# Score units of a head pair side by side in six PSUM banks, transposes over four banks, Q and K projected together

## What is computed

```python
h = layernorm(x) * (1 + ca) + sa
q, k, v = h @ W_Q, h @ W_K, h @ W_V              # 16 heads of 64
probs = softmax(where(causal, -1e6, q @ k.T / 8))
x = x + ga * ((probs @ v) @ W_out + b_out)
h = layernorm(x) * (1 + cb) + sb
x = x + gb * top2_of_8_experts(h)                # 128 -> 512 -> 128, gelu
```

## Time and profile before

| what | value |
|---|---|
| median of three runs | 2189.81 us (2189.57 to 2190.14) |
| profiled execution | 2190.27 us, span 2188.5 us |
| TensorE busy | 2047.3 us, 94% of the span |
| VectorE busy | 1700.8 us, 78% |
| ScalarE busy | 1531.4 us, 70% |
| GpSimd busy | 722.2 us, 33% |
| granted TensorE clock, mean | 0.994 |

### The profile page before, as it was taken

How to read it: one execution, slowest core, us unless ns; L and a number is a source line. 1 busy time by engine, 2 the same in 40 slices (tenths; PEclk the granted TensorE clock), 3 DMA queues, 4 the chain that set the end, 5 groups by cost and what they waited for, 6 DMA issues and landing times. The chain is left out here.

```text
span 2188.5 us, 45861 instructions
## 1 busy us (share of the span) xinstructions
PE 2047.3 (94%) x12751; PEld 1550.8 (71%) x12751; DVE 1700.8 (78%) x4517; ACT 1531.4 (70%) x3749; POOL 722.2 (33%) x1215
## 2 busy tenths in 40 slices
PE   5999999999999999999999999879999999999998
PEld 3676666666666666667666667568888888888887
DVE  5877767777777677777777777579999888898887
ACT  4777667667677676676677767567776777676775
POOL 2334334333333333333343434212222222222222
PEclk9999999999999999999999999989999999999999
DMA  3000000000000000000000000031211112111111
GB/s 109 16 1 1 0 1 1 0 0 1 0 1 0 1 1 0 1 1 0 1 0 0 1 0 1 1 116 47 75 50 47 43 43 69 56 48 43 43 47 45
DMA packets 41996, 49.99 MB, mean 23 GB/s; under 512 B 3176, under 2 KB 23712, under 8 KB 41888
## 3 DMA queue, kind: packets, MB, share of 16 engines
q1 hardware_dynamic: 41632, 48.41, 7.0%
q0 software_dynamic: 256, 0.53, 0.1%
HBM read 44.47 MB, written 4.46 MB: 22 GB/s over the span
## 5 line engine op out<-in xcount | busy, mean ns | idle before, releaser
L340 POOL TENSOR_SCALAR probs<-probs,rdenom 128x512 f32<-128x512 f32 (+3 forms) x1024 | 522.4, 532 | 840.6 <-DVE rdenom L694 840.6
L564 ACT ACTIVATE probs<-probs,neg_max 128x512 f32<-128x512 f32 (+3 forms) x1024 | 562.8, 553 | 287.2 <-DVE neg_max L685 287.2
L685 DVE CUSTOM_DVE_ANT_0 probs<-banks,mask_w 128x512 f32<-128x512 f32 (+3 forms) x1024 | 441.0, 485 | 66.7 <-PE banks L398 53.5
L1005 ACT ACTIVATE hidden<-banks,b_cols 128x512 f32<-128x512 f32 x512 | 348.4, 685 | 198.5 <-PE banks L871 172.9
L1124 DVE TENSOR_TENSOR hid_lo<-hidden,hid_hi 128x512 fp32r<-128x512 f32 x512 | 386.7, 763 | 67.5 <-ACT hid_hi L1013 55.2
L427 PE MATMUL banks<-ident,probs 128*128 128x128 f32 x2560 | 392.2, 280 | 46.4 <-DVE z_lo L698 34.0
L427 PEld LDWEIGHTS banks<-ident,probs 128*128 128x128 f32 x2560 | 289.7, 141 | 154.0 <-DVE probs_T L674 50.7
L943 POOL TENSOR_TENSOR acc<-acc,y_w 128x512 f32<-128x512 f32 x112 | 155.1, 1385 | 489.5 <-DVE y_w L1137 489.5
L439 PE MATMUL banks<-probs_T,v_sb 128*64 128x512 f32 (+3 forms) x2048 | 303.9, 439 | 1.6 <-DVE probs_T L674 1.6
L674 DVE COPY probs_T<-banks 128x512 f32<-128x512 f32 x384 | 261.7, 681 | 55.4 <-PE banks L427 54.6
L439 PEld LDWEIGHTS banks<-probs_T,v_sb 128*64 128x64 f32 x2048 | 136.0, 137 | 152.4 <-issue 124.2
(11 more groups left out here) (138 smaller groups left out, 3506.2 us busy)
## 6 DMA issues: line engine op xcount, KB each, us to landing
w_rows<-w_kept SPq DMA_DIRECT2D x128, 256.0 KB, 3.9
x_all<-in_L_attn_resid_dram SPq DMA_DIRECT2D x16, 256.0 KB, 2.6
out_dram<-y_result SPq DMA_DIRECT2D x16, 256.0 KB, 2.3
w_raw<-in_L_ffn_W_dram SPq DMA_DIRECT2D x12, 256.0 KB, 4.0
hidden<-in_L_ffn_W_dram SPq DMA_DIRECT2D x4, 256.0 KB, 6.3
v_sb<-in_L_attn_W_Q_dram SPq DMA_DIRECT2D x1, 512.0 KB, 6.0
v_sb<-in_L_attn_W_K_dram SPq DMA_DIRECT2D x1, 512.0 KB, 8.1
v_sb<-in_L_attn_W_V_dram SPq DMA_DIRECT2D x1, 512.0 KB, 11.2
```

Of the source, the lines that this page charges most:

```text
L340: pool.tensor_scalar(part, part, rdenom[:, p % 2, 4 * h + r:4 * h + r + 1], 1.0, ALU.mult, ALU.mult)\
L564: act.activation(part, part, ACT.Exp, bias=neg_max[:, p % 2, col:col + 1], scale=-1.0, accum_out=denom[:, p % 2, col:col + 1]).then_inc(p_ ...
L685: dve.tensor_tensor_reduce(out=probs[:, p % 2, h, at:at + n], in0=s_banks[S_BANK[u] + h][:, col:col + n], in1=mask_w[:, 512 - n:512], scal ...
L1005: act.activation(hidden[:, e % 2, c, :], banks[:, c, :], ACT.Gelu, bias=b1_cols[:, e * HC + c:e * HC + c + 1]).then_inc(hid, 1)
```

## The change

The three score units of a pair get six banks of their own: unit 0 `s_banks[0:2]`, unit 1 `s_banks[2:4]`, unit 2 `z_bank` and `g_bank`. The transposes go in turn over four banks: T0 `g_bank`, T1 `s_banks[0]`, T2 `s_banks[1]`, T3 `z_bank`, T4 `g_bank`. The order on TensorE in a pair becomes: unit 0, unit 2, unit 1, weighting, [output projection], T0, Q, K, [attention_T], T1, T2, V, T3, V, T4. VectorE masks unit 2, then 0, then 1, and ScalarE takes the exponentials in that order; q_lo and k_lo, and q_hi and k_hi, stand next to each other. The V chunks move: pair 2 has none, pair 5 has one. The waits follow the banks: scores wait for the copies of the transposes, transposes T0 to T2 and the weighting for the masks of the pair under way.

```diff
-S_BANK = [0, 2, 0]
-V_CHUNKS = [[0, 1], [2, 3], [4], [5, 6], [7], [], [], []]
+V_CHUNKS = [[0, 1], [2, 3], [], [4, 5], [6], [7], [], []]
-    return (h, 2 + 2 * h, 6 + h)[u]
+    return (2 + h, 4 + 2 * h, h)[u]
-        T_BANK = [g_bank, z_bank, g_bank, z_bank, g_bank]
+        T_BANK = [g_bank, s_banks[0], s_banks[1], z_bank, g_bank]
+        S_BANK = [s_banks[0:2], s_banks[2:4], [z_bank, g_bank]]
...
# TensorE, scores(b, p, u, begin, young)
+                            if not young:
+                                pe.wait_ge(t_act, pair(2, b, p) - 3)
+                                pe.wait_ge(t_dve, pair(3, b, p) - 4)
-                        if u == 2:
-                            pe.wait_ge(s_masked, pair(8, b, p) + 2)
+                        if u == 2 and not young:
+                            pe.wait_ge(t_act, pair(2, b, p) - 2)
+                            pe.wait_ge(t_dve, pair(3, b, p) - 3)
...
# TensorE, transposes(b, p, u, begin, step)
-                        if u == 0 and not begin:
-                            pe.wait_ge(t_dve, pair(3, b, p))
-                        if u == 1 and not begin:
+                        if u < 3 and step is not None:
+                            pe.wait_ge(s_masked, pair(8, *step) + 2 + u)
+                        if u == 3 and not begin:
                             pe.wait_ge(z_done, pair(1, b, p))
-                        if u == 2:
+                        if u == 4:
                             pe.wait_ge(t_dve, pair(3, b, p) + 1)
-                        if u == 3:
-                            pe.wait_ge(t_act, pair(2, b, p) + 1)
-                        if u == 4:
-                            pe.wait_ge(t_dve, pair(3, b, p) + 2)
...
# TensorE, the body of a pair
-                            scores(b, p, 0, begin)
+                            scores(b, p, 0, begin, young)
+                            scores(b, p, 2, begin, young)
...
-                            scores(b, p, 1, begin)
+                            scores(b, p, 1, begin, young)
+                            if not young:
+                                weigh_values(*prev2, (b, p))
                             if p == 2 and not first:
                                 project_out(b - 1)
-                            if not (first and p < 2):
-                                weigh_values(*prev2)
-                            scores(b, p, 2, begin)
...
                             if not begin:
-                                transposes(*prev, 0, first and p == 1)
+                                transposes(*prev, 0, young, (b, p))
                             if has_next:
                                 project_q(*nxt)
-                            if not begin:
-                                transposes(*prev, 1, first and p == 1)
...
                             if has_next:
                                 project_k(*nxt)
+                            if p == 4 and not first:
+                                attention_T(b - 1, pair(8, b, p) + 8)
                             if not begin:
-                                transposes(*prev, 2, False)
+                                transposes(*prev, 1, young, (b, p))
+                                transposes(*prev, 2, young, (b, p))
...
# ScalarE, the body of a pair
-                            exponentials(b, p, 0, 0)
-                            exponentials(b, p, 1, 0)
+                            for u in (2, 0):
+                                for h in range(2):
+                                    exponentials(b, p, h, u)
...
# VectorE, the body of a pair
-                            mask_and_max(b, p, 0, early)
-                            mask_and_max(b, p, 1, early)
+                            for u in (2, 0, 1):
+                                mask_and_max(b, p, u, early)
...
-                            mask_and_max(b, p, 2, early)
                             if not begin:
                                 evac_T(*prev, 0, first and p == 1)
                             if has_next:
                                 rest_q(*nxt)
+                                rest_k(*nxt)
+                            if p == 4 and not first:
+                                add_attention(b - 1)
                             if not begin:
                                 evac_T(*prev, 2, False)
-                            if has_next:
-                                rest_k(*nxt)
```

More of the change, by code:

```diff
@@ L375, in h_transposes, with scores @@
                         for t in range(NT):
-                            mm = pe.transpose(s_banks[2][:, t * P:(t + 1) * P], xn[:, t, :], ident[:, :])
+                            mm = pe.transpose(s_banks[3][:, t * P:(t + 1) * P], xn[:, t, :], ident[:, :])
                         mm.then_inc(lnT_ps, 1)
-                    def scores(b, p, u, begin):
+                    def scores(b, p, u, begin, young):
                         if u == 0:
@@ L397, in scores @@
                                     own = slice(h * DH, (h + 1) * DH)
-                                    mm = pe.matmul(s_banks[S_BANK[u] + h][:, at:at + n], q[own, p % 2, rows],
+                                    mm = pe.matmul(S_BANK[u][h][:, at:at + n], q[own, p % 2, rows],
                                                    k[own, p % 2, 0:n], start=start, stop=stop)
@@ L407, in _, with transposes @@
                                [(h, 2, r, 256 * h + (r - 2) * P) for h in range(2) for r in (2, 3)]]
-                    def transposes(b, p, u, begin):
+                    def transposes(b, p, u, begin, step=None):
                         if u == 0:
@@ L428, in transposes, with weigh_values @@
                         mm.then_inc(t_ps, 1)
-                    def weigh_values(b, p):
+                    def weigh_values(b, p, step=None):
+                        if step is not None:
+                            pe.wait_ge(s_masked, pair(8, *step) + 1)
                         pe.wait_ge(t_dve, pair(3, b, p) + 3)
@@ L446, in values @@
                         t, half = i % 4, i // 4
-                        pe.wait_ge(s_masked, pair(8, b, p) + 6)
+                        pe.wait_ge(s_masked, pair(8, b, p) + 8)
                         toks, cols = slice(t * P, (t + 1) * P), slice(half * 512, half * 512 + 512)
@@ L477, in body @@
                         for p in range(NP):
[L478 removed]
+                            begin, young = first and p == 0, first and p < 2
                             has_next = not (last and p == NP - 1)
                             prev, prev2, nxt = before(b, p), two_before(b, p), after(b, p)
[L481 removed]
+                            scores(b, p, 0, begin, young)
+                            scores(b, p, 2, begin, young)
                             if p > 0 and V_CHUNKS[p - 1]:
@@ L509, in body @@
                             if p == 5 and not last:
-                                pe.wait_ge(s_masked, pair(8, b, p) + 6)
+                                pe.wait_ge(s_masked, pair(8, b, p) + 8)
                                 h_transposes(b + 1)
                             if not begin:
-                                transposes(*prev, 3, False)
+                                transposes(*prev, 3, young, (b, p))
                             if len(V_CHUNKS[p]) > 1:
                                 values(b, p, 1)
-                            if p == 4 and not first:
-                                attention_T(b - 1, pair(8, b, p) + 6)
                             if not begin:
-                                transposes(*prev, 4, False)
+                                transposes(*prev, 4, young, (b, p))
                     end = B - 1
@@ L676, in mask_and_max @@
                     def mask_and_max(b, p, u, early):
-                        if u == 0 and not early:
+                        if u == 2 and not early:
                             wait_alone(dve, t_ps, pair(5, b, p) - 5)
-                        wait_alone(dve, s_ps, pair(3, b, p) + u + 1)
+                        wait_alone(dve, s_ps, pair(3, b, p) + (1, 3, 2)[u])
                         for h in range(2):
@@ L727, in body @@
                             has_next = not (last and p == NP - 1)
-                            mask_and_max(b, p, 0, early)
-                            mask_and_max(b, p, 1, early)
+                            for u in (2, 0, 1):
+                                mask_and_max(b, p, u, early)
                             if p == 2 and not first:
                                 gate_attention(b - 1)
-                            if not (first and p < 2):
+                            if not early:
                                 rest_z(*two_before(b, p))
-                            mask_and_max(b, p, 2, early)
                             if not begin:
@@ L747, in body @@
                                 evac_T(*prev, 4, False)
-                            if p == 4 and not first:
-                                add_attention(b - 1)
```

16 lines of the change are left out of this document (7 added, 9 removed).

## The result

The changed kernel takes 2155.24 us (median of four, 2151.86 to 2161.79); the kernel before, run beside it, took 2189.97 (2189.57 to 2191.0). The ratio is 0.9842 [0.9822, 0.9861]: faster by 34.7 us, where 15.9 were forecast, and the time lies under the lower end of the range. The sign and the waits came out as written; the size is off by more than half.

A forecast was written before the change was run, and what follows sets the result against it. TensorE's work was taken to bound pairs with V, a chain over three engines those without. Savings of 12.6 us in the loop, 0.9 in the unrolled batches and 2.4 in the drain total 15.9, giving 2174 us, range 2158 to 2198.

The forecast's parts named there:

- TensorE's own work: TensorE in every pair: moving score units and weighting costs nothing by itself; a pair with two V chunks takes 9.76 us.
- The jump: Pair 0: VectorE's first mask (M) starts 2.30 us after its last copy, 2.83 after unit 0's start (S); pair 0 takes 10.90.
- The release and the mask's start: Pair boundary: waits release in 0.14 us (ends 0.04, 0.24); first mask starts 0.22 after unit 2's issue, up to 0.32.
- z_lo's hole: TensorE before transposes: the 34.0 us wait goes, as z_hi and z_lo get more than two us of cover.
- the waits for k_lo: TensorE before scores, 31.9 us: K is projected before T1, so k_lo is never late because of TensorE.
- The slots of the chain: ScalarE and VectorE, from a pair's first mask (M): q_hi at M+5.31, k_lo M+6.54, T4's copy ends M+8.51.
- Pair 4: Next batch's normalisation ahead of the masks, residual sum (0.61) before T2's copy: first mask at 2.54, pair 11.13 us.
- the normalisation: VectorE in pair 4, ahead of the masks: the next batch's normalisation takes 1.91 us in four pieces.
- The longer chain: Rival, slower: the mask-to-copy round of pairs 2, 4, 5, 6, 7 and the jump exceeds its slots; 0.35 gives 2204; chance 0.14.
- the rival of no change: Rival at the pair boundary: release 0.24 and mask start 0.32 together take 18 us, giving 2185 to 2194; chance 0.15.
- TensorE's work bounds all: Rival, much faster: k_lo and copies never late, pairs 6 and 7 take 8.32; 73 us less, 2116; chance 0.05.
- The clock: Rival: holes in and before pair 0 drop TensorE's clock to 0.52, costing 27 us over fourteen batches: 2201; chance 0.06.

The follow-up runs named there:

- the two moves together: Layer norm into VectorE's holes and pair 4's residual sum behind T4's copy, against the changed kernel: 2133.89 us, ratio 0.9747 to the kernel before.
- the last kernel: On the two moves together: h's subtraction behind T4's copy in pair 6, T4 ahead of the second V chunk; 2117.14 us, ratio 0.9662 to the kernel before.

## Why the prediction was right in kind and wrong in size

**TensorE's own work: the step that failed, a cost put at nothing.** "Moving them costs nothing by itself: the number and size of the instructions stay." They stay, and their cost doesn't. Pair 3 of the change has two V chunks and no hole worth the name, as pair 1 had before (K of that pair, and what follows it, in the first two lines; then the change):

```profile
643.99 0.48 PE L350 MATMUL banks<-h_hi,wk_hi 128*128 128x512 f32 x1
...
644.78 0.66 PE L427 MATMUL banks<-ident,probs 128*128 128x128 f32 x4
```

```profile
654.11 0.50 PE L403 MATMUL banks<-k_hi,q_hi 64*128 64x512 f32 x2 [0.26 <-DVE probs_T L677]
...
654.91 0.29 PE L403 MATMUL banks<-k_hi,q_hi 64*128 64x256 f32 x2
...
655.26 0.35 PE L403 MATMUL banks<-k_hi,q_hi 64*128 64x384 f32 x2
...
658.89 0.48 PE L350 MATMUL banks<-h_hi,wq_hi 128*128 128x512 f32 x1
...
659.66 0.40 PE L350 MATMUL banks<-h_hi,wk_hi 128*128 128x512 f32 x1
...
660.36 1.03 PE L429 MATMUL banks<-ident,probs 128*128 128x128 f32 x8
...
663.60 0.49 PE L403 MATMUL banks<-k_hi,q_hi 64*128 64x512 f32 x2
```

It takes 9.49 (654.11 to 663.60), not 9.76. Unit 2 between the weighting and T0 held TensorE for 0.54; straight behind unit 0 it holds it for 0.35 (654.91 to 655.26). K held it for 0.79 behind T1 (643.99 to 644.78); straight behind Q it is 0.70 (659.66 to 660.36). T1 and T2 side by side save nothing (0.79 for both, 0.77 apart). That is 0.19 + 0.07 = 0.26, the whole of the pair's gain.

One run parts the two. With T1 between Q and K again, TensorE's order differs from that of the kernel before only in unit 2, and pair 3 took 9.57: 0.07 more than in the change, 0.19 less than before. The banks differ as well there, so the 0.19 is not tied to the order alone. And the fall of 32.8 in busy time can't be put down to this: 0.26 in 128 pairs would be 33, but the run that gives 0.07 a pair back was busy for 2008.8 us, less than the change run again (2010.9). Only in a pair that TensorE bounds does the whole of it reach the time.

What the forecast missed, pair by pair, is 0.44 in pair 0, 0.01 in pair 1, 0.19 in pair 2, 0.26 in pair 3, and 0.17, 0.28 and 0.10 in pairs 5 to 7, less 0.12 in pair 4: 1.33 a batch. Pair 3 is TensorE's work; pair 0 is mostly the jump.

**The jump: the largest term that was mis-sized.** "At the loop's jump VectorE starts its first mask 2.30 after its last copy." The number was right and hung on the wrong event. Counted from T4's end it is 3.28 to 3.43 in the three jumps shown, and the change has T4 done 1.19 before the next unit 0. The first mask comes at S+2.24 and not S+2.83, and pair 0 takes 10.46, not 10.90. The release behind it went the other way: the weighting starts 0.77 after M, where 0.56 was taken; in pairs 2 and 4 the same wait ends 0.48 after M, and why the two differ stays open. The weighting at 3.01 in place of 3.39, and 7.45 in place of 7.51 behind it, are the 0.44.

**The release and the mask's start.** Unit 0 starts 0.05 to 0.06 after a copy, not 0.14. And since unit 2 issues faster, the first mask of a chain-bound pair starts at S+1.47, where 0.79 + 0.54 + 0.22 = 1.55 was taken; the forecast let its start be wrong upwards only. A chain-bound pair is 1.47 + 7.87 = 9.34, not 9.53: pairs 5, 6 and 7 got 0.17, 0.28 and 0.10 less than forecast.

**What was right.** z_lo's hole went, and of the waits for k_lo one of 1.5 us was left. The slots of the chain held to 0.02, in all pairs but 2 and 4, where other work stands in it. Pair 1 (9.90 against 9.91) did so by two errors that cancel: the weighting starts at 2.48, not 2.40, with 7.42 behind it, not 7.51. Pair 4 stays the worst of the new waits, because normalisation and residual sum lie on the chain: the forecast priced it at 11.13, and the two moves together took 1.7 of it away. Its one term that came out longer is the normalisation: 1.91 was taken and 2.17 measured, so the first mask came at 2.79 and not 2.54.

**The rivals.** The longer chain fell: but for the normalisation each of its terms came out equal or shorter. So did the rival of no change, which hung on a release of 0.24. "TensorE's work bounds all" was right that there was more to win, and wrong on where. It took pairs 6 and 7 at 8.32; even the last kernel has them at 9.51 and 9.35.

**The clock** fell, but in single pairs: three times in the loop of the profiled execution. The first of them starts in pair 7 and leads to the second (TensorE's weighting in that pair 7, VectorE's first mask and TensorE's weighting in the pair 0 behind it, then windows as above):

```profile
269.31 3.61 PE L444 MATMUL banks<-probs_T,v_sb 128*64 128x512 f32 x16
```

```profile
280.20 0.42 DVE L688 CUSTOM_DVE_ANT_0 probs<-banks,mask_w 128x256 f32<-128x256 f32 x1 [2.59 <-issue]
```

```profile
280.97 1.56 PE L444 MATMUL banks<-probs_T,v_sb 128*64 128x512 f32 x6 [1.83 <-DVE neg_max L688]
```

```profile
268.00:272.00 4.00, 4.00 (x24) 2.17 (x22) 3.38 (x16) 3.19 (x11) 3.20 (x7) 0.57 0.00 0
277.00:281.00 4.00, 2.16 (x26) 1.85 (x26) 1.41 (x7) 0.33 (x1) 3.78 (x8) 1.00 0.01 4
281.00:285.00 4.00, 4.00 (x19) 2.09 (x20) 2.58 (x12) 3.67 (x14) 0.30 (x1) 0.64 0.01 2
```

In this pair 7 TensorE stood for 1.18 us before unit 0, as in every batch, and then ran at a granted clock of 0.57, part of it at 1.2 GHz: the weighting took 3.61 in place of 2.37 and the pair 10.70 in place of 9.92. T4 was done only 0.34 before the next unit 0, not 1.19, so the first mask came late (3.54 behind T4), TensorE stood for 1.83 us, and the clock fell again: pair 0 took 13.03. The other pair 7 of this kind (10.69) left a hole of 1.56, behind which the clock stayed at 1.00, and its pair 0 took 11.16. This late T4 is what makes VectorE late in these two. The kernel before has no hole over 1.23 in its loop and not one such stretch there, which fits its spread (1.4 us against 10). The last kernel, with the same four banks in turn, has none in its loop either, so the turn over the banks is not what brings it.

The rival took the fall in all fourteen batches or in none. The length of a hole did not decide it alone: 1.2 us before unit 0 of pair 7 was followed by it in two of fourteen batches, and with two banks for the transposes 1.81 to 2.00 us in six of thirteen. What does decide stays open.

## What to carry to other kernels

Price a reordering of TensorE's work by the issue time of each group behind its new neighbour: here a short scores unit issued 0.19 us faster behind another one, a projection 0.09 faster behind a projection, and a pair without holes became 0.26 shorter, where nothing had been forecast. Tie a delay to the event that starts it by comparing two places where the candidates lie apart, before it is carried into a sum. And where a chain over engines bounds a stage, look at what else stands in it: moving layer norm, a residual sum and a subtraction off the chain, and T4 ahead of a V chunk, gave 40 us on top of the change's 35.

## What the runs showed of the hardware that was not expected

- A 128x128 normalisation on VectorE took 341 to 346 ns alone and, in the change, 430 to 754 beside GpSimd's scaling of probabilities. The four of one batch took 2.17 us there, in other kernels 1.59 in some batches, and the whole pair followed this step of 0.6. The masks, which read a PSUM bank, kept their 0.42 and 0.69 there. The Trainium skill (SBUF — State Buffer, "Who interferes with whom") says that VectorE and GpSimd share a port pair under an exclusive lock. The most that was added to one tile is 0.41 us, less than one of GpSimd's instructions (4.08 us for eight), so these rows agree with a lock held for one instruction; no run tells it from sharing.
- VectorE's first instruction of the next turn of the loop started 3.28 or 3.43 us after the release of the last wait of the turn before in the three jumps shown, with two or three instructions between; over all jumps of the kernels with one batch in the body it was 3.25 to 4.03.
- With a loop body twice as long TensorE stood for 2.7 to 3.8 us at each of the six jumps; behind the one of 3.63 a granted clock of 0.56 followed.
- Behind a hole of 1.2 us in pair 7 the granted clock fell in two of fourteen batches (0.57 in the stretch shown) and stayed at 1.00 in the other twelve.
